# A two-layer set of LSTMs: PSUM redivided into an ordered pair of buffers and one for the forget gate, loads and h exchange put in another order

## What is computed

```python
def step(carry, xt):
    h, c = carry
    g = xt @ Wx + h @ Wh + b
    i, f, gg, o = jnp.split(g, 4, axis=-1)
    c = sigmoid(f) * c + sigmoid(i) * tanh(gg)
    h = sigmoid(o) * tanh(c)
m_from = lstm_last(base_emb[from_seq], seq_Wx, seq_Wh, seq_b)   # 64 steps, H = 64
m_to   = lstm_last(base_emb[to_seq],   seq_Wx, seq_Wh, seq_b)
nwf = vmap(enc)(...)              # 11 features, 32 steps, H = 8, tables of 1000 rows
y = relu(concat([goby, bools, m_from, m_to, counts, nwf]) @ reduce_W + reduce_b)
```

## Time and profile before

| what | value |
|---|---|
| median of 3 runs | 2191.85 us (2182.32 to 2198.21) |
| the profiled execution | 2191.35 us |
| its span, first to last instruction | 2189.6 us |
| granted TensorE clock, mean over the span | 0.967 |

### The profile page before, as it was taken

How to read it: one execution, slowest core, us unless ns; L and a number is a source line. 1 busy time by engine, 2 the same in 40 slices (tenths; PEclk the granted TensorE clock), 3 DMA queues, 4 the chain that set the end, 5 groups by cost and what they waited for, 6 DMA issues and landing times. The chain is left out here.

```text
span 2189.6 us, 63997 instructions
## 1 busy us (share of the span) xinstructions
PE 1806.4 (83%) x27396; PEld 767.8 (35%) x27396; DVE 1672.6 (76%) x1284; ACT 1076.4 (49%) x1459; POOL 1083.3 (49%) x477
## 2 busy tenths in 40 slices
PE   2278788888888888888888888888888888888884
PEld 1123333333333333333333333333333333333333
DVE  7178878887878787877788778888788877888771
ACT  2235455555545555555555545555455554555541
POOL 7358754545444445444444544544454444454551
PEclk9589999999999999999999999999999999999996
DMA  6789899999989999999999898899989998999962
GB/s 171 178 244 273 272 283 282 290 302 286 284 284 284 289 282 291 282 287 285 277 287 288 280 281 285 292 283 288 272 286 303 284 285 274 298 287 288 296 217 52
DMA packets 248101, 593.97 MB, mean 271 GB/s; under 512 B 56036, under 2 KB 158220, under 8 KB 206860
## 3 DMA queue, kind: packets, MB, share of 16 engines
q1 hardware_dynamic: 245259, 589.73, 87.0%
q0 software_dynamic: 2560, 0.15, 0.8%
HBM read 536.95 MB, written 7.54 MB: 249 GB/s over the span
## 5 line engine op out<-in xcount | busy, mean ns | idle before, releaser
L612 ACT ACTIVATE gate<-g_ps 128x1024 f32<-128x1024 f32 (+1 forms) x768 | 710.9, 940 | 232.9 <-PE g_ps L565 229.5
L645 POOL TENSOR_TENSOR seq_h<-gate,tanh_c 128x1024 f32<-128x1024 f32 x128 | 382.6, 2989 | 713.3 <-ACT tanh_c L639 713.2
L503 PE MATMUL e_ps<-hot,tab 128*32 128x512 bf16 x8448 | 531.6, 387 | 221.6 <-DVE hot L493 216.7
L493 DVE TENSOR_SCALAR hot<-low,cst 128x4096 bf16<-128x4096 bf16 x352 | 559.1, 1588 | 0.1
L512 DVE SCALAR_TENSOR_TENSOR kept<-high,cst,e_ps 128x1024 f32<-128x1024 bf16 x352 | 447.9, 1273 | 120.3 <-issue 106.7
L565 PE MATMUL g_ps<-seq_h,seq_wh 64*64 64x512 f32 x4096 | 535.5, 596 | 0.0
L619 POOL TENSOR_TENSOR ig<-gate 128x1024 f32<-128x1024 f32 x192 | 445.5, 2320 | 74.3 <-ACT gate L612 74.3
L503 PEld LDWEIGHTS e_ps<-hot,tab 128*32 128x32 bf16 x8448 | 195.3, 97 | 639.2 <-DVE hot L493 452.5
L459 DVE TENSOR_SCALAR seq_hot<-tok,cst 128x2048 bf16<-128x2048 bf16 x128 | 249.5, 1950 | 167.2 <-DMA tok<-seq_tokens 167.1
L538 ACT COPY nwf_x<-x_ps 128x256 f32<-128x256 f32 (+1 forms) x192 | 68.0, 354 | 505.0 <-PE x_ps L529 505.0
L473 ACT CAST seq_x<-sx_ps 128x512 bf16<-128x512 f32 x256 | 150.6, 588 | 250.1 <-PE sx_ps L467 248.9
(11 more groups left out here) (68 smaller groups left out, 981.7 us busy)
## 6 DMA issues: line engine op xcount, KB each, us to landing
low<-low_digits SPq DMA_DIRECT2D x352, 1024.0 KB, 8.0
high<-high_digits SPq DMA_DIRECT2D x1408, 64.0 KB
tok<-seq_tokens SPq DMA_DIRECT2D x128, 512.0 KB, 5.5
seq_h<-seq_h SPq DMA_DIRECT2D x256, 128.0 KB, 2.9
nwf_h<-nwf_h SPq DMA_DIRECT2D x64, 128.0 KB, 2.6
nwf_h<-nwf_h SPq DMA_DIRECT2D x64, 48.0 KB, 4.8
nwf_in<-in_r_nwf_numbers SPq DMA_DIRECT2D x1, 2816.0 KB, 13.7
nwf_in<-in_r_nwf_freqs SPq DMA_DIRECT2D x1, 2816.0 KB, 20.9
```

The lines of the kernel that those rows point to most:

```text
L493: nc.vector.tensor_scalar(hot[:, p % HOT_RING, :, :].rearrange("p u c -> p (u c)"), low[:, p % LOW_RING, :, :].rearrange("p u c -> p (u c) ...
L503: last = nc.tensor.matmul(e_ps[32 * g:32 * g + 32, i, :], tab[:, part, 2 * m + ty, :], hot[:, p % HOT_RING, i, g * CH:(g + 1) * CH], start ...
L612: nc.scalar.activation(gates[g][:, n % 2, 0:2 * w].rearrange("p (b c) -> p b c", b=2), g_ps[g % 2][:, :, 0:w], GATES[g][1]).then_inc(gate_ ...
L645: nc.gpsimd.tensor_tensor(h_blocks(n)[:, 0:2, :].rearrange("p b c -> p (b c)"), gates[3][:, n % 2, 0:w], tanh_c[:, n % 2, 0:w], ALU.mult). ...
```

## The change

1. PSUM: `g_ps`, `x_ps` and `sx_ps` go. In their place are `ab`, two buffers of two banks used strictly in turn by everything in the list `USES` (inputs of a feature set, gates g, i and o, token look-ups), and `f_ps`, two banks, for gate f. A use waits until the one two before it has been evacuated (`begin_use`). ACT makes the sigmoid of f in place in `f_ps`; DVE's `scale_c` writes c*f there and `add_c` reads it there. So gate f of cell n waits until `add_c` of cell n - 1 is done.
2. `bring` per pair becomes `set_input` per feature set, in the cell after its last pair, with the same matmuls. The token look-up is one step of four matmuls and one copy 1024 wide, in place of two of each. `AHEAD` goes from 4 to 2.
3. Orders: PE does the first look-up of a cell before its gates and the last one between f and o. DVE compares a pair further ahead and does the last `keep_wanted` of a cell in that cell. ACT does tanh of cell n - 1 after gate g of cell n. POOL's order stays: h of cell n - 1, then i*g of cell n.
4. Loads: `high_dram` is laid out so that both units of a pair and its four parts come with one DMA, 2 KB to each of 128 partitions. The `high` ring is 4, `kept` 4. Units are stored so that each pair's `low` is one run. SP issues pairs three ahead; tokens are issued at the end of a seq cell, two seq cells ahead of their compare.
5. In the head each of the two stores of high digits is 8 DMAs in place of 4.

```diff
-LOW_RING, HIGH_RING, HOT_RING, KEPT_RING, X_RING = 3, 3, 2, 2, 6
-AHEAD = 4
+AHEAD, X_RING = 2, 3
+LOW_RING, HIGH_RING, HOT_RING, KEPT_RING = 3, 4, 2, 4
+USES = [("sx", _s) for _s in range(AHEAD)]
+for _n in range(NCELLS):
+    USES += [("x", _r, _m) for _r, _m in SETS_AT[_n]]
+    USES += [("gate", _n, 0), ("gate", _n, 1), ("gate", _n, 3)]
+    if later_seq(_n) is not None:
+        USES.append(("sx", later_seq(_n)))
...
-        STORES = [2] * 2 + [4] * 4
+        STORES = [2] * 2 + [4, 8] * 2
...
-        g_ps = [work.enter_context(nc.psum_tensor(f"g_ps{n}", [P, 2, CH], F32)) for n in range(2)]
+        ab = [work.enter_context(nc.psum_tensor(f"ab{n}", [P, 2, CH], F32)) for n in range(2)]
+        f_ps = work.enter_context(nc.psum_tensor("f_ps", [P, 2, CH], F32))
         e_ps = work.enter_context(nc.psum_tensor("e_ps", [P, 2, CH], F32))
-        x_ps = work.enter_context(nc.psum_tensor("x_ps", [P, 256], F32))
-        sx_ps = work.enter_context(nc.psum_tensor("sx_ps", [P, CH], F32))
...
+        def begin_use(pe, what):
+            at_least(pe, ab_done, USE[what] - 1)
+            return ab[USE[what] % 2]
...
             at_least(sp, kept_ready, p - HIGH_RING + 1)
-            for g in range(4):
-                sp.dma_start(high[32 * g:32 * g + 32, p % HIGH_RING, :, :],
-                             high_dram[step:step + 1, both, g, :]
-                             .to_broadcast([32, 2, CH])).then_inc(high_here[p % HIGH_RING], 16)
+            sp.dma_start(high[:, p % HIGH_RING, :, :].rearrange("p u c -> p (u c)"),
+                         high_dram[step, k, :, None, :, :].rearrange("g o u c -> g o (u c)")
+                         .to_broadcast([4, 32, 2 * CH])).then_inc(high_here[p % HIGH_RING], 16)
...
-            at_least(pe, gate_done, 4 * n + g - 1)
+            if g == FORGET:
+                at_least(pe, c_ready, n)
+                bank = f_ps
+            else:
+                bank = begin_use(pe, ("gate", n, g))
...
+        def activate_f(act, n):
+            w = width(n)
+            act.wait_ge(f_ready, n + 1)
+            nc.scalar.activation(f_ps[:, :, 0:w], f_ps[:, :, 0:w], GATES[FORGET][1]).then_inc(f_done, 1)
...
-            nc.vector.tensor_tensor(c_of(n), c_of(n), gates[2][:, n % 2, 0:w], ALU.mult).then_inc(c_scaled, 1)
+            nc.vector.tensor_tensor(f_ps[:, :, 0:w], by_blocks(c_of(n), n), f_ps[:, :, 0:w],
+                                    ALU.mult).then_inc(c_scaled, 1)
...
-            nc.vector.tensor_tensor(c_of(n), c_of(n), ig[:, n % 2, 0:w], ALU.add).then_inc(c_ready, 1)
+            nc.vector.tensor_tensor(by_blocks(c_of(n), n), by_blocks(ig[:, n % 2, 0:2 * w], n), f_ps[:, :, 0:w],
+                                    ALU.add).then_inc(c_ready, 1)
...
                 for n in range(NCELLS):
-                    if n:
-                        tanh_of(act, n - 1)
+                    for r, m in SETS_AT[n]:
+                        store_x(act, r, m)
                     activate(act, n, 0)
+                    if n:
+                        tanh_of(act, n - 1)
                     activate(act, n, 1)
...
                     pairs = PAIRS_AT[n]
-                    gate(pe, n, 0)
-                    gate(pe, n, 1)
                     for p in pairs[:1]:
                         look_up(pe, p)
+                    for r, m in SETS_AT[n]:
+                        set_input(pe, r, m)
+                    gate(pe, n, 0)
+                    for p in pairs[1:-1]:
+                        look_up(pe, p)
+                    gate(pe, n, 1)
+                    gate(pe, n, FORGET)
+                    if len(pairs) > 1:
+                        look_up(pe, pairs[-1])
+                    gate(pe, n, 3)
```

More of the change, by code:

```diff
@@ L49 @@
 GATES = [(2, ACT.Tanh), (0, ACT.Sigmoid), (1, ACT.Sigmoid), (3, ACT.Sigmoid)]
+FORGET = 2
 PAIRS = []
@@ L389, in build @@
         kept = sb("kept", [P, KEPT_RING, 2, CH], F32, work)
-        gates = [sb(f"gate{g}", [P, 2, 2 * CH], F32, work) for g in range(4)]
+        gates = {g: sb(f"gate{g}", [P, 2, 2 * CH], F32, work) for g in (0, 1, 3)}
         ig = sb("ig", [P, 2, 2 * CH], F32, work)
@@ L476, in load_pair, with seq_store_x @@
+            last.then_inc(ab_ready, 1)
+        def seq_store_x(act, s):
+            act.wait_ge(ab_ready, USE["sx", s] + 1)
+            nc.scalar.copy(seq_x[:, s % X_RING, :, :], ab[USE["sx", s] % 2][:, :, :]).then_inc(ab_done, 1)
         def load_pair(sp, p):
             step, j = divmod(p, NPAIRS)
-            one, other = [stored_as(u) for u in PAIRS[j]]
-            both = slice(one, other + 1, other - one)
+            k = stored_pair(j)
             at_least(sp, hot_ready, p - LOW_RING + 1)
@@ L800, in _ @@
                 for s in range(AHEAD):
-                    for q in range(2):
-                        seq_lookup(pe, s, q)
+                    seq_lookup(pe, s)
                 pe.wait_ge(state_set, 1)
```

238 lines of the change are left out of this document (118 added, 120 removed).

## The result

| | before | after |
|---|---|---|
| median, in the same comparison | 2195.03 us (2182.32 to 2204.92) | 2729.68 us (2719.35 to 2751.86) |
| ratio to before, 95% interval | 1 | 1.2453 (1.2351 to 1.2555) |
| span of the profiled execution | 2189.6 us | 2726.1 us |
| a round | 63.1 us | 80.5 us |

A forecast was written before the change was run, and what follows sets the result against it. VectorE's chain was taken as the bound, 8.3 us of its 63.1 us round being waits for loads. 63.1 - 8.3 + 0.8 + 2.3 + 0.5 = 58.4; 2191.35 - 146 + 2 = 2047, given as 2050 us, range 1930 to 2150.

The forecast's parts named there:

- the same bytes, but `high` differently cut: DMA demand, 58.1 us a round, falls by 0 to 4.3 us with the new `high`; adds nothing to the sum.
- The mask's "issue" wait: VectorE's wait before a mask, taken as a wait for `high`: 3.3 us a round, to go with the ring of 4.
- Tokens: VectorE's wait for token loads, 5.0 us a round, goes when they are issued two seq cells ahead.
- What the token wait hid: Token compares on VectorE stand behind GpSimd's product of h once their load is early: +2.3 us a round, at most 4.6.
- Rows 10: Profile rows of before: GpSimd product and token compare overlap, one stands still while the other works; 1.22 us lost per compare.
- Waits for loads that stay: VectorE still waits for loads, `low` the tight one, as SP stands at the h exchange: +0.8 us a round, at most 8.3.
- PSUM operands: c*f and the addition on VectorE have one operand in PSUM, priced by the mask's time: +0.5 us a round.
- Gate f, turns of PSUM and tanh: VectorE's new wait for i*g, at most +4.5 us a round, cancels the vanished gate f wait, -4.0; taken as 0.
- Head: Four more stores of high digits before the barrier: +2 us once, between 0 and 5.0.
- DMA takes over: Rival, also the DMA rival: DMA engines at share 0.95 bound the round at 61.2 us, 2130 us in all; chance 0.14.
- Slower, by shared access: Rival: VectorE sits out one more GpSimd product of h per seq cell, round 65.6 us, 2270 us; chance 0.11.

The follow-up runs named there:

- e1: The changed kernel with each `high` load as four DMAs of 32 partitions in place of one: 2182.69 us, ratio 0.9893 to the kernel before.
- e7: e1 with only the first unit of each `low` loaded, the other zeros, so half of the look-ups is missing from the result: 2049.18 us, ratio 0.9309.
- e8: The kernel before with tokens issued at the end of a seq cell, two seq cells ahead, and a `high` ring of 4: 2154.92 us, ratio 0.9776.
- e5: e1 with ScalarE's tanh of the cell before moved ahead of gate g again: 2234.56 us, ratio 1.0161.
- e6: e1 with rings of 4 for `low` and 5 for `high`, in place of 3 and 4: 2163.36 us, ratio 0.9853.
- e2: e1 with SP issuing the h exchange behind both pairs of the cell instead of between them: 2193.18 us, ratio 0.9934.
- e4: The kernel before with the new DRAM layout of `high`, 2 KB rows, still loaded by four DMAs: 2193.24 us, ratio 0.995.
- e11: e8 with the 2 KB rows of `high` of e4, still four DMAs: 2144.44 us, ratio 0.9725.

## Why the prediction was wrong, step by step

VectorE's round, each column from that kernel's stretch and waits above, divided by its rounds (us):

| | before | after | e1 | e7 | e8 | forecast |
|---|---|---|---|---|---|---|
| busy | 50.4 | 47.0 | 48.8 | 47.5 | 52.4 | 53.2 |
| waits for tokens | 5.0 | 0 | 0 | 0 | 0 | 0 |
| waits for `low` | 0 | 27.6 | 3.8 | 0.3 | 0.4 | 0.8 |
| mask behind its look-up | 3.4 | 2.1 | 6.2 | 5.4 | 4.1 | 0.1 |
| f and i*g | 4.0 | 3.6 | 4.5 | 5.2 | 4.4 | 4.0 |
| round | 63.1 | 80.5 | 63.4 | 58.5 | 61.7 | 58.4 |

**The step that failed: "the same bytes, but `high` differently cut".** The DMA term was bounded by 0 and -4.3 us a round and entered the sum as nothing, as though a DMA's cut could only help. It measured +17.1 (80.5 in after against 63.4 in e1). The sum treated 16 engines as one pipe with a mean share, and a share of 0.92 as room; the new `high` runs on four of them. The line in the diff, `.to_broadcast([4, 32, 2 * CH])`, shows a 4 where `low` and the old `high` had 128 and 32; with it the working above gives 66 to 86 us a round from rows of before.

**The mask's "issue" wait, -3.3.** Wrong. It was given to `high` since the look-up had only 3.2 us to its name; it is a wait for the look-up. The kernel before, TensorE and VectorE, and then SP's issue of this mask's `high`:

```profile
902.41 1.48 PE L503 MATMUL e_ps<-hot,tab 128*32 128x512 bf16 x24
...
904.00 1.28 DVE L512 SCALAR_TENSOR_TENSOR kept<-high,cst,e_ps 128x1024 f32<-128x1024 bf16 x1 [3.71 <-issue]
```
```profile
886.61 1.73 SPq L486 DMA_DIRECT2D high<-high_digits  x4
```

The look-up ends at 903.89 and the mask starts 0.11 us later; `high` had been issued 17 us earlier, and by its increments landed 8.7 us earlier. 41 of the mask's 42 waits of over 0.4 us in this trace, 35 of the 36 marked "issue" among them, end within 0.2 us behind a look-up, and so do 112 of 113 in e1 (200 to 1900 us). In the new order the wait grew to 6.2 us a round. The likely reason is TensorE's order, in which the cell's last look-up stands behind g, i and f; no run moves it. The same in e1 (TensorE, VectorE):

```profile
1009.99 1.48 PE L549 MATMUL e_ps<-hot,tab 128*32 128x512 bf16 x24
...
1011.58 1.28 DVE L561 SCALAR_TENSOR_TENSOR kept<-high,cst,e_ps 128x1024 f32<-128x1024 bf16 x1 [1.72 <-issue]
```

**Tokens, -5.0.** Right as a wait: it is gone in after, e1 and e8. As a gain it was too large: in e8 alone 1.4 us remain of it.

**What the token wait hid, +2.3.** Right in kind where tokens alone move (2.5 in e8, of which 1.6 at the token compare, to which the prediction gave all). In the new order it has the other sign: busy time fell by 1.6 us in e1, the token compare to 1722 ns and the pair compare to 1497, since tanh behind gate g takes about half of the products out of the compares' way (e5). Rows 10 were read rightly; that the new order would keep the collisions was an assumption.

**Waits for loads that stay, +0.8.** Too small: 3.8 in e1. The DMA rival had this right: at a share of 0.90 to 1.00 the new order has no slack for `low`; a deeper ring halves the wait (e6) and fewer bytes end it (e7). That SP behind the h exchange makes it was the reason given for it; e2 does not bear it out.

**PSUM operands, +0.5.** It measured nothing. c*f and the sum in after, 200 to 2600 us, against 1211 and 1225 ns:

```profile
L693 DVE TENSOR_TENSOR seq_c<-ig,f_ps 128x1024 f32<-128x1024 f32 x119 | 145.3, 1221 | 4.7 <-POOL ig L675 0.7
L686 DVE TENSOR_TENSOR f_ps<-seq_c,f_ps 128x1024 f32<-128x1024 f32 x119 | 145.1, 1220 | 0.0
```

The mask was the nearest row that read PSUM, and what it takes beyond 1225 ns is not the price of that.

**Gate f, turns of PSUM and tanh, 0.** Right as a sum: +3.8 for i*g in e1 (4.5 was the bound), -3.3 for gate f. But 2.4 of the 3.8 lie in nwf cells, and the working was for seq cells.

**Head, +2.** Not contradicted, but outweighed. With the same stores in the old order the first narrow tanh comes 4.4 us later in e4 than before, and 0.5 later in e11 than in e8; in e1 it comes 8.3 earlier than before, which the stores can't have given.

Corrected, e1's column is 63.1 - 5.0 + 3.8 + 2.8 - 1.6 + 0.5 = 63.6 against 63.4 measured: apart from the cut of `high`, gains and losses of the change cancel, and the range of 1930 to 2150 us would have missed e1's 2182.69 too.

**The rivals.** "DMA takes over" named the right resource and put the round at 61.2 us, not 80.5, since it kept the mean over 16 engines. "Slower, by shared access" had the right sign and a mechanism that is not in the changed kernel: its token compare takes 990 ns in the mean, and its product of h 2368, about the shortest of before (2365).

**What stays open.** Whether a better order of TensorE would take the mask's wait (6.2 us a round in e1) away was not tried, nor was a `low` ring of 4 in the old order without the shorter `AHEAD`. That the four engines of one `high` are the four of the next is taken from the twelve early and four late increments of `low`; no record names an engine.
